# Router logits of a four-block gated transformer: gate halves side by side, 16 instead of 24 matmuls a call, and a VectorE sum of two column groups

## The reference, cut to what matters

```
# part 1: E = 8, TOP_K = 2  (part 0: E = 8, K = 2, and a sigmoid gate
# for the shared expert; part 3: E = 16, K = 6)
probs = jax.nn.softmax(xf @ router_w, axis=-1)
topk_vals, topk_ids = jax.lax.top_k(probs, TOP_K)
combine = zeros((N, E)).at[arange(N)[:, None], topk_ids].add(topk_vals)
...
routed = jnp.einsum('ne,end->nd', combine, y)
```

## Time and profile before

| what | value |
|---|---|
| median of 3 runs | 1122.41 us (1118.03 to 1123.39) |
| the profiled execution's own time | 1120.06 us |
| its span, first to last instruction | 1118.3 us |
| TensorE busy | 1001.5 us, 90% |
| VectorE, ScalarE, GpSimd busy | 731.0, 580.6, 408.5 us |
| mean granted TensorE clock | 0.953 of full speed |

### The profile page before, as it was taken

The page is one execution under the profiler, slowest core; times in us unless marked ns, Lnnn a source line. Parts: engine busy times, 40 slices in busy tenths (PEclk is TensorE's granted clock), DMA queues, the critical chain, the costliest instruction groups (busy, mean ns, idle before and its releaser), DMA issues.

```text
span 1118.3 us, 18120 instructions
## 1 busy us (share of the span) xinstructions
PE 1001.5 (90%) x6456; PEld 760.5 (68%) x6456; DVE 731.0 (65%) x1629; ACT 580.6 (52%) x1129; POOL 408.5 (37%) x521
## 2 busy tenths in 40 slices
PE   3899878998988998789999776799999899999997
PEld 2666546787877887565664575566555588888886
DVE  6467755757867556778888666876676365445444
ACT  3688853454533554236667442265565545554553
POOL 5524403445414445432223035324210144444452
PEclk9899978999998999879999998899999899999999
DMA  7955714465530468945521255734521244556553
GB/s 178 245 109 123 170 36 129 137 169 156 156 108 1 117 175 187 171 85 125 130 54 41 76 128 123 153 91 85 123 48 33 61 138 124 158 139 184 159 154 102
DMA packets 82067, 136.54 MB, mean 122 GB/s; under 512 B 11565, under 2 KB 40518, under 8 KB 79546
## 3 DMA queue, kind: packets, MB, share of 16 engines
q1 hardware_dynamic: 71034, 101.93, 31.4%
q0 software_dynamic: 10944, 33.45, 17.3%
HBM read 113.41 MB, written 22.97 MB: 122 GB/s over the span
## 4 chain that ended last, share of the span: by engine, by line
PE 65%; DVE 16%; ACT 5%; DMA 5%; POOL 4%; issue 4%; SPq 1%; DVEq 0%; ACTq 0%; POOLq 0%
PE psum L621 42%; PE psum L914 7%; PE psum L881 6%; PE psum L890 5%; ACT probs L1063 2%; DMA ff_w<-weights_out 2%; PE psum L840 1%; DVE nmx L1379 1%; DVE nmx L1376 1%; DVE nmx L1377 1%; POOL keys L1126 1%; PE psum L722 1%; DVE probs L1470 1%; POOL ff_wl L1937 1%; DMA keys<-keys_out 1%
## 5 line engine op out<-in xcount | busy, mean ns | idle before, releaser
L621 PE MATMUL psum<-ff_xh,ff_wh 128*128 128x512 f32 x424 | 173.7, 410 | 20.0 <-POOL ff_wl L1937 13.6
L1065 ACT ACTIVATE probs<-psum 128x512 f32<-128x512 f32 x256 | 144.4, 597 | 78.7 <-PE psum L881 75.1
L881 PE MATMUL psum<-queries,keys 128*128 128x512 f32 x384 | 157.8, 441 | 12.9 <-ACT probs L1063 5.8
L1937 POOL TENSOR_TENSOR ff_wl<-ff_raw,ff_wh 128x512 fp32r<-128x512 f32 x92 | 118.8, 1291 | 100.6 <-ACT ff_wh L1889 100.6
L621 PE MATMUL psum<-ff_xh,ff_wl 128*128 128x512 f32 x392 | 155.0, 395 | 0.0
L890 PE MATMUL psum<-keys,queries 128*128 128x512 f32 x256 | 117.9, 477 | 17.0 <-DVE nmx L1377 8.2
L621 PE MATMUL psum<-ff_wh,ff_hh 128*128 128x256 f32 x456 | 128.9, 286 | 4.1 <-DVE ff_hl L1992 3.9
L621 PE MATMUL psum<-ff_wh,ff_hl 128*128 128x256 f32 x456 | 128.5, 286 | 0.0
L1982 DVE TENSOR_TENSOR psum<-ff_s,psum 128x512 f32<-128x512 f32 x98 | 68.2, 696 | 86.8 <-PE psum L621 85.7
L914 PE MATMUL psum<-probs,values 128*32 128x256 f32 x1664 | 112.1, 392 | 2.9 <-DVE probs L1470 2.7
L1942 POOL TENSOR_TENSOR ff_wl<-ff_raw,ff_wh 128x256 fp32r<-128x256 f32 x92 | 69.7, 758 | 122.8 <-ACT ff_wh L1896 122.7
(11 more groups left out here) (271 smaller groups left out, 2194.4 us busy)
## 6 DMA issues: line engine op xcount, KB each, us to landing
ff_w<-weights_out SPq DMA_DIRECT2D x94, 256.0 KB
ff_raw<-in_ff SPq DMA_DIRECT2D x92, 256.0 KB, 4.1
ff_raw<-in_ff SPq DMA_DIRECT2D x106, 128.0 KB, 2.1
keys_out<-keys_turned SPq DMA_DIRECT2D x24, 512.0 KB, 3.7
keys<-keys_out POOLq DMA_DIRECT2D x48, 256.0 KB, 5.1
queries_out<-queries_turned SPq DMA_DIRECT2D x24, 256.0 KB, 4.4
keys<-keys_out POOLq DMA_DIRECT2D x48, 128.0 KB, 5.4
queries<-queries_out POOLq DMA_DIRECT2D x32, 192.0 KB, 3.7
```

What stands on the lines that cost most here:

```text
L621: last = eng.matmul(dst, lhs[i](k), rhs[j](k), start=start and n == 0, stop=stop and n == groups * len(pairs) - 1, skip_group_check=True)
L881: then(eng.matmul(dst, kst[buf(c)][:, pair, kt * P:(kt + 1) * P], qst[buf(c)][:, :, pair, :], start=True, stop=True, skip_group_check=True ...
L1065: ins = eng.activation(dst, src, ACT.Exp, scale=SCALE)
L1937: then(eng.tensor_tensor(ff_wl[:, slot, 0:2 * D], raw(n)[:, 0:2 * D], ff_wh[:, slot, 0:2 * D].bitcast(F32), ALU.subtract), "f_w1r")
```

## The change

The rounded gate and its rest are written next to each other in one buffer, `gate_hl`: columns 0 to EL-1 the rounded part, EL to 2 EL-1 the rest. For each token tile and each block of the contraction, one matmul takes the rounded tokens against all 2 EL columns, and a second takes the rest of the tokens against the first EL columns. PSUM then holds two column groups a token tile. A new VectorE reduction adds the two groups into `rt_o` in SBUF; the maximum, the subtraction and (in part 0) ScalarE's exponential of the shared column read `rt_o`. Only EL gate columns are split instead of 16. `gate_hl` lies at `rt`, where the unused `rt_l` was, and `gate_hi` no longer takes bytes of its own, so what is allocated behind it moves down by 128 bytes a partition.

```diff
-    rt_l = at("rt_l", rt, [P, T, 16])
...
-    gate_lo = at("gate_lo", rt + 3264, [P, KC, 16], F32R)
     gate_raw = sb("gate_raw", [P, KC, 16])
-    gate_hi = sb("gate_hi", [P, KC, 16], F32R)
+    gate_hl = at("gate_hl", rt, [P, KC, 32], F32R)
...
-                then(eng.activation(gate_hi[:, :, :], gate_raw[:, :, :], ACT.Copy), "f_gh")
+                then(eng.activation(gate_hl[:, :, 0:self.EL], gate_raw[:, :, 0:self.EL], ACT.Copy), "f_gh")
...
-                then(eng.tensor_tensor(gate_lo[:, :, :], gate_raw[:, :, :], gate_hi[:, :, :].bitcast(F32),
+                n = self.EL
+                then(eng.tensor_tensor(gate_hl[:, :, n:2 * n], gate_raw[:, :, 0:n], gate_hl[:, :, 0:n].bitcast(F32),
                                        ALU.subtract), "f_gl")
...
-                last = passes(eng, psum[:, bank, t * n:(t + 1) * n],
-                              [lambda c: xh[:, c, cols], lambda c: xl[:, c, cols]],
-                              [lambda c: gate_hi[:, c, 0:n], lambda c: gate_lo[:, c, 0:n]])
+                for c in range(KC):
+                    eng.matmul(psum[:, bank, 2 * t * n:2 * (t + 1) * n], xh[:, c, cols], gate_hl[:, c, 0:2 * n],
+                               start=c == 0, stop=c == KC - 1, skip_group_check=True)
+                    last = eng.matmul(psum[:, bank, 2 * t * n:(2 * t + 1) * n], xl[:, c, cols], gate_hl[:, c, 0:n],
+                                      start=False, stop=c == KC - 1, skip_group_check=True)
...
-            return psum[:, bank, 0:4 * self.EL].rearrange("p (t e) -> p t e", e=self.EL)
+            return psum[:, bank, 0:8 * self.EL].rearrange("p (t g e) -> p t e g", g=2, e=self.EL)
...
-                eng.activation(rt_c[:, ts, self.E], self.got(bank)[:, :, self.E], ACT.Exp, scale=-1.0)
+                eng.activation(rt_c[:, ts, self.E], rt_o[:, ts, self.E], ACT.Exp, scale=-1.0)
...
-                dl(eng.tensor_reduce(rt_s[:, 0, ts], self.got(bank)[:, :, 0:E], AX.X, ALU.max))
-                then(eng.tensor_tensor(p_, self.got(bank)[:, :, 0:E], spread(0), ALU.subtract), "f_re")
+                dl(eng.tensor_reduce(rt_o[:, ts, 0:self.EL], self.got(bank), AX.X, ALU.add))
+                dl(eng.tensor_reduce(rt_s[:, 0, ts], rt_o[:, ts, 0:E], AX.X, ALU.max))
+                then(eng.tensor_tensor(p_, rt_o[:, ts, 0:E], spread(0), ALU.subtract), "f_re")
```

## The result

The changed kernel takes 1113.58 us, the median of 13 runs (1109.07 to 1118.32), against 1122.43 for the kernel before, timed beside it (13 runs, 1114.0 to 1125.62). The ratio is 0.9929, 95% interval 0.9910 to 0.9948. It is beyond the 0.5% bound, and on the upper side of what the terms gave.

What follows compares the result with a forecast made beforehand. TensorE was taken to bound the kernel (65% of the chain), weight loads pacing its narrow logits matmuls. Calls 4.8 us plus clock 1.4 us made 6.2 us, off 1121.2: forecast 1115.0 us, range 1111.0 to 1120.5.

Steps and rivals of the forecast that it cites:

- The pace of the wide matmul: In each logits call, the paired matmul of 16 to 32 columns was to cost 0.11 us, set by its weight load.
- The sum's duration: The added VectorE reduction in each logits call was to take about 225 to 290 ns.
- Its place: The added VectorE sum was to lie on the path only in first-half calls of parts 0 (0.27 us) and 1 (0.25 us).
- two tiles of `down` lag: In the three second-half calls, this lag was to hide the sum's delay, costed at nothing; uncovered it would be 0.84 us.
- one step: Part 1, first half: VectorE's statistics feed GpSimd's root, whose following tile releases TensorE, so the call gives 0.88 - 0.25 = 0.63 us.
- The calls' term: Six logits calls, eight load-and-matmul pairs fewer each (0.88 us), less the sum where on the path: 4.8 us saved.
- The clock's term: Behind part 1 first-half and part 3 second-half calls, half-clock stretches might vanish, worth 2.8 us; half was taken, 1.4 us.
- The clock gives all: Rival: 4.8 + 2.8 us, plus 2.4 us from falls after attention-side calls; 10.0 us in all, 1111.2 us; chance 0.13.
- Caught up: Rival: attention stages absorb their savings, only second-half calls keep theirs, clock gives nothing; 2.4 us, 1118.8 us; chance 0.29.
- Two slots: Rival: the paired matmul costs 0.22 us, saving nothing on TensorE, while VectorE's chain gains 0.5 us; 1121.7 us; chance 0.05.
- The sign turned: Rival: attention stages of parts 0 and 3 take further half-clock stretches, 1.6 us each; seven more give 1127.6 us; chance 0.05.
- the 112, 136 and 160 matmuls: Expected sign in the profile after: TensorE pieces of the chain with these counts where there were 120, 144 and 168.

## Why the prediction was right, and where it was off

**The pace of the wide matmul** was right: 0.11 to 0.12 us with 20 to 32 columns, 1.8 us a call. The landmarks of the two second-half calls without a fall give 0.87 and 0.84 us a call, 8 x 0.107. The 81 ns a pair of the Trainium skill ("TensorE: Matmul & The Clock Gate", section "Back-to-back issue gap") would make it 0.65, as an estimate, and the trace doesn't bear that out.

**The sum's duration** was right: 216 to 291 ns against 225 to 290. **Its place** was right for one sum: the chain of after has it in the two calls that I named, the second-half calls gave their full 0.87 and 0.84, and the call of part 0, first half, gave 0.58 for 0.61. The reason that I gave for the second-half calls, two tiles of `down` lag, was not the one that counts: with five sums the delay came, in parts 1 and 3, through ScalarE's exponential and the next tile's rounding, at 0.6 us a sum over the three second-half calls. In part 1, first half, one step was misread: in the kernel before, GpSimd's tile waited for ScalarE's rounding behind TensorE's own slowed piece, and not for the root. The chain of before there:

```profile
363.38 0.46 ACT psum L1902
...
364.35 0.62 ACT ff_wh L1889
...
365.04 1.28 POOL ff_wl L1937
```

Only in the kernel after does the root carry the chain there. So without the clock that call would have given 0.88, not 0.63; with it, the root sets 1.8, and 1.76 was measured. The lower fixed cost of SBUF operands that the Trainium skill's "VectorE: DVE Perf Modes" states (section "The TRN2 errata — SBUF-src ops pay a fixed extra latency per instruction") did not show: in the kernel after, the maximum reads SBUF in 186 ns, against 192 from PSUM.

**The calls' term**, 4.8 us, is confirmed where it stands alone (0.87, 0.84, 0.58). With the clock held up by wide matmuls, pairing gave 3.1 us for it; that is lower, but inside the uncertainty.

**The clock's term was mis-sized.** I took 1.4 us, half of 2.8; the mean clocks put it at 3 to 4, the table of narrow and wide at 5.6. Three parts of the step failed. I counted two of the four falls of the earlier trace rows, though the fall in part 3, first half, turned out worth 2.55 - 0.88 = 1.7 us by its landmarks: I had taken attention as too alternating for the clock to matter. I took the profiled execution's falls as the number to be removed; over many profiles a 24-matmul call is followed by one in 15 of 21 cases, also behind calls that had none in that profile. And I halved the sum for doubt whether shorter calls would help, where 3 of 30 against 15 of 21 says that they nearly always do. 4.8 + 4 = 8.8 us would have met the 8 measured. How the gain divides between loads and clock is known only to some 2 us: 4.8 and 4 by the landmarks and the clocks, 3.1 and 5.6 by the table.

**The rivals.** "The clock gives all" (10.0) was 2.0 us above the measured 8.0, the forecast of 6.2 was 1.8 below it; the two can't be told apart by the time, and in mechanism the rival was nearer on part 3, first half (1.7 us for its 1.6), and wrong on part 0, first half (nothing for 0.8). "Caught up" (2.4) fell: it lies outside the interval of 5.8 to 10.1. "Two slots" fell with the pace. "The sign turned" fell too: falls did come at new places (315.0), but the mean clock rose from 0.9565 to 0.9606. The chain of after has the 112, 136 and 160 matmuls that were forecast between its landmarks.

**Luck.** The forecast of 1115.0 is 1.4 us above the 1113.58 measured, nearer than the gain was. The base of 1121.2, a median of four executions, was 1.2 us below the 1122.43 of thirteen, and that took as much off an error in the gain of 2.7 us between the medians.

## What to carry to other kernels

Before counting matmuls, look at what the granted clock does behind a run of narrow ones in the middle of dense work: here its price was about as large as that of the loads removed, and some or all of it came back with three quite different edits (fewer, wider, or split in two). The moving operand repeated by a broadcast to 128 columns cost 0.04 us a call of 24. Repeating a step several times to price it holds only while its cover lasts: look in the chain whether it has come onto the path. Where executions differ by the falls of the clock, compare two profiles by distances between landmarks, never by positions, and count over many profiles before pricing a fall.

## What the runs showed of the hardware

Widening each of 144 matmuls from 8 to 16 columns up to 128, with not one load less, made the kernel 7.6 us faster (0.9928 and 0.9937), which I had not expected of doing more work. Falls to half clock followed 15 of 21 runs of 24 narrow matmuls, 3 of 30 of 16 narrow ones, 2 of 12 of 24 wide ones and none of three that were split; widening, shortening and splitting each make them rarer. Why is not shown. Both falls behind wide calls are in part 1, first half, behind a wait of TensorE of 1.4 us. The stretches at half clock elsewhere, some 14 to 21 us between 450 and 500 us and 20 to 31 between 600 and 730, are in every profile, with any of these kernels.
